# Gathers of the last three layers of a graph network: one wait for a free buffer in place of waits spread over the batch

## The chip, the cores and the metric

The kernel runs on one core of a Trainium2 chip. The metric is device time in microseconds (us). The engines: PE is TensorE (PEld its weight loads), DVE is VectorE, ACT is ScalarE, POOL is GpSimd, SP is SyncE. Engines have queues of their own and are ordered by semaphores alone: `wait_ge(S, n)` holds an engine's queue until semaphore S is at least n, and `then_inc(S, 1)` raises S when the instruction is done. Where this text says that PE *signals*, it means such a raise.

## The reference

Four layers of a graph network over 6250 nodes with 256 features and 106250 edges, sorted by the node that receives. Each layer is x = x + layer(relu(layernorm(x))). Cut to what matters:

```
L0: messages from x[src], edge_attr_4 and an MLP of edge_attr_16; segment_sum; polynomial; batch norm
L1: sums = segment_sum((x @ W_src)[src], dst); mean by degree; batch norm; relu
L2: xp = x @ W;  alpha = leaky_relu(a_src[src] + a_dst[dst] + a_edge);  softmax of alpha over dst
    out = segment_sum(xp[src] * attn, dst); residual; layer norm
L3: the same without a_edge, self loops handled apart
```

What counts here is the step that L1, L2 and L3 share: for each edge a row of a table of nodes is fetched from HBM (the gather), and rows are summed by receiving node.

## The kernel before, in words

Edges are laid out in 880 steps of 128 (`ST`). One indirect DMA on POOL's queue fetches the 128 rows of one step: rows of 256 floats in layer 1 (`k.table`), of 264 floats in layers 2 and 3 (`k.sender_rows`, 8 heads of 32 values and a score). Each layer has 880 such gathers.

**Layer 1, `aggregate` (tag g1).** 110 batches of 8 steps; index, row and one-hot buffers fourfold. PE per batch (`multiply`, L902): transposes edge attributes (`turn`), waits for the one-hot matrices (`sel`) and for all 8 gathers, multiplies one-hot by rows in two halves of four steps (`sums`; L898 and L895). The first half signals `ha`, the second half with the attribute product L887 signals `hb`. DVE (`add`, L975) waits `ha`, adds four steps into `acc`, waits `hb`, adds four. ACT waits `ha` for L923 and `hb` for L929, and makes the one-hot matrices of the batch two further on. PE may not write a half of `psA` again before DVE has added it.

**Layers 2 and 3, `gat` (tags g2, g3).** 55 batches of 16 steps; rows and indices threefold. A body for batch t computes the softmax of t while the sums of batch t-1 are interleaved, a quarter (four steps) at a time. The chain of one body:

- DVE `score` (L2020 to L2024) waits for the 16 gathers of t (`ga`) and for PE's product `sp` (L1874, `spread`, made at the end of the body before). It makes z.
- PE `turn` (L1899) transposes z and signals `zt`; DVE `within` makes running maxima `loc`; PE `edges_of` (L1904, L1905) signals `tb`; ACT and DVE go over the steps (`between`); PE `columns` (L1910) signals `cc`; DVE `differ` makes df; PE `back` (L1926) transposes it and signals `dt`; right after it PE makes `spread` for t+1 and signals `sp`.
- ACT exponentiates (L1994, L1995, after `dt`), DVE weighs the rows (L2088) and goes to `score` of t+1.
- PE's queue in order: sums q0 of t-1, turn, sums q1, edges, sums q2, columns, sums q3, factors, back, spread. So `zt`, `tb`, `cc`, `dt` also say that a quarter of t-1 has been summed. The last reader of the rows of batch t-3 is its sums q3, which `dt` at t-1 covers.

**POOL, layer 1** (`gather`, L861): waits for its indices; before step 0 waits `ha` at t-1, before step 4 `hb` at t-1, that is, until PE has done the first and the second half of batch t-2. **POOL, layers 2 and 3** (`gather`, L1850): before step 0 waits `dt` at t-1; before steps 5, 7 and 9 waits `zt`, `tb`, `cc` at t, which come from body t-1. Each wait is followed by an increment of `go`, for which nobody waits. Buffers that were never used need no wait.

SP's queue loads the indices and, in `gat`, the broadcast rows `bc`, the lines and the heads, each behind its own wait (L1828 to L1844).

Of the kernel before, what the change touches and what calls it, by code (L numbers as in the profile page):

```python
# [93 lines left out]
def triples(eng, times, body):  # L94

    for b in range(3):
        body(b, b, 0)
    with eng.Fori(1, times // 3) as i:
        for b in range(3):
            body(i * 3 + b, b, i)  # L100
    body(times - 1, 0, times // 3)
# [36 lines left out]
def later(i):  # L138

    return not isinstance(i, int) or i > 0  # L140
# [7 lines left out]
def reach(eng, sem, value):  # L148

    if not isinstance(value, int) or value > 0:  # L150
        eng.wait_ge(sem, value)
# [630 lines left out]
def aggregate(nc, k, tag, w_e, att_edge):  # L782
# [8 lines left out]
    with es:  # L791
        S = {n: s[tag + n] for n in names + ["gat0", "gat1", "gat2", "gat3"]}
# [8 lines left out]
        Q = U2 // 2  # L801
# [21 lines left out]
        def eras(eng, body):  # L823

            for t in range(AGE):
                body(t, t, 0, True)
            with eng.Fori(1, (NF - 1) // AGE) as i:
                for c in range(AGE):
                    body(i * AGE + c, c, i, True)
            for t in range((NF - 1) // AGE * AGE, NB2):  # L830
                body(t, t % AGE, t // AGE, t < NF)

        def turns(c, i):

            return i * (AGE // 4) + c // 4

        @block.sync
        def _(sp):
            for o in (0, 1):
                sp.dma_start(we[o * C:(o + 1) * C, :], w_e).then_inc(S["w"], 16)  # L840
            sp.dma_start(av[:, :], att_edge.rearrange("h c -> (h c)").partition_broadcast(P)).then_inc(S["w"], 16)

            def load(t, c, i, left):
                b, n = c % 4, turns(c, i)
                if later(n):
                    sp.wait_ge(r_sem[b], n * per)
                sp.dma_start(idx[b][:, :], k.src_of[:, ds(t * U2, U2)]).then_inc(i_sem[b], 16)
                if left and later(n):
                    sp.wait_ge(S["ha"], t - 3)
                if left and not (isinstance(t, int) and t == NF - 1):  # L850
                    sp.dma_start(f[b][:, :, :], tiles(k.attr[ds(t * (EU * P), EU * P), :])).then_inc(f_sem[b], 16)
                elif left:
                    whole = FT - t * EU
                    sp.dma_start(f[b][:, 0:whole, :], tiles(k.attr[t * EU * P:FT * P, :])).then_inc(f_sem[b], 16)
                    sp.dma_start(f[b][0:LE, whole, :], k.attr[FT * P:E, :]).then_inc(f_sem[b], 16)

            eras(sp, load)

        @block.gpsimd
        def _(g):  # L860
            def gather(t, c, i, left):  # L861
                b, n = c % 4, turns(c, i)
                g.wait_ge(i_sem[b], n * 16 + 16)
                for u in range(U2):
                    if u % Q == 0:
                        if later(n):
                            g.wait_ge(S["hb" if u else "ha"], t - 1)
                        g.sem_inc(S["go"], 1)
                    g.indirect_dma_start(rows[b][:, u, 0:D], None, k.table,  # L869
                                         bass.IndirectOffsetOnAxis(ap=idx[b][:, u:u + 1], axis=0)  # L870
                                         ).then_inc(r_sem[b], 16)

            eras(g, gather)
# [879 lines left out]
def gat(nc, k, tag, edge, own):  # L1753
# [14 lines left out]
    with es:  # L1768
        S = {n: s[tag + n] for n in names + ["ga0", "ga1", "ga2"]}
# [3 lines left out]
        Q = U // 4  # L1773
        HALF = RW // 2

        def sb(name, shape, dt=F32):
            return es.enter_context(nc.sbuf_tensor(tag + name, shape, dt))
# [22 lines left out]
        tb = sb("tb", [1, H, K])  # L1800
# [25 lines left out]
        @block.sync  # L1826
        def _(sp):
            def load(t, b, i):  # L1828
                if later(i):
                    sp.wait_ge(gas[b], i * full)  # L1830
                sp.dma_start(idx[b][:, :], k.src_of[:, ds(t * U, U)]).then_inc(ix[b], 16)
                reach(sp, S["oh"], t)
                sp.dma_start(bc[:, :], k.dst_rows[ds(t * U, U)].rearrange("t e -> (t e)").partition_broadcast(P)
                             ).then_inc(S["bc"], 16)
                if later(i):
                    sp.wait_ge(S["d"], t - 2)
                sp.dma_start(ln[b][:, 0:LU], k.lines[ds(t * U, U), 0:LU].unsqueeze(0).broadcast_to([H, U, LU])
                             ).then_inc(lns[b], 16)
                if edge:
                    sp.dma_start(ae[b][:, :], k.edge_steps[ds(t * U, U), :].rearrange("u (h e) -> h u e", h=H)  # L1840
                                 ).then_inc(aes[b], 16)
                if later(i):
                    sp.wait_ge(S["dt"], t - 2)
                sp.dma_start(hd[b][:, :], k.heads[ds(t, 1), :]).then_inc(hds[b], 16)  # L1844

            triples(sp, NB, load)

        @block.gpsimd
        def _(g):
            def gather(t, b, i):  # L1850
                g.wait_ge(ix[b], i * 16 + 16)
                behind = {0: S["dt"], 5: S["zt"], 7: S["tb"], 9: S["cc"]}
                for u in range(U):
                    if u in behind:
                        reach(g, behind[u], t if u else t - 1)
                        g.sem_inc(S["go"], 1)
                    g.indirect_dma_start(rows[b][:, u, 0:TW], None, k.sender_rows,  # L1857
                                         bass.IndirectOffsetOnAxis(ap=idx[b][:, u:u + 1], axis=0)
                                         ).then_inc(gas[b], 16)

            triples(g, NB, gather)
# [585 lines left out]
```

## Time and profile before

| | us |
|---|---|
| median of 3 runs | 6624.06 (6608.26 to 6634.96) |
| span of the profiled execution | 6720.7 |

The runs' times are taken without the profiler. For the profiled execution the span is the time that is given; it lies 96.6 us (1.5%) above the median.

| engine | busy us | share of the span |
|---|---|---|
| PE | 4346.5 | 65% |
| DVE | 3982.7 | 59% |
| POOL | 3443.0 | 51% |
| PEld | 3322.6 | 49% |
| ACT | 3104.0 | 46% |

How to read the rows below: a row of a timeline is the start in us from the span's start, the duration in us, engine, source line, operation, out<-in, how many instructions it merges, and in brackets how long the engine had been idle before and what ended that. "remote", and the name of a DMA that has nothing to do with the wait, both mean that the wait ended so long after the raising instruction that the profile doesn't connect them. The duration of a POOL row is the time POOL took to hand over the gather, not the transfer.

### The profile page before, as it was taken

The numbers are of one execution on the slowest core, as the hardware profiler recorded it, in microseconds if no ns is written. First come the engines' busy times: TensorE is split into PE (matmuls) and PEld (weight loads), VectorE is DVE, ScalarE is ACT, GpSimd is POOL, SyncE is SP. The second block draws the span as 40 slices with busy tenths as digits, with TensorE's granted clock in tenths as the row PEclk, the third lists the DMA queues.
The fourth block names the chain that finished last, engine by engine and source line by source line (L and its number), as shares of the span: only waits on it lengthen the run. The fifth ranks groups of instructions, "written<-read, shape, count | busy, mean of one in ns | idle before, by whom it ended". The sixth has DMA issues, their size and how long they took to land. (4 is left out here: it accounts for less than half of the span.)

```text
span 6720.7 us, 90392 instructions
## 1 busy us (share of the span) xinstructions
PE 4346.5 (65%) x22227; PEld 3322.6 (49%) x22228; DVE 3982.7 (59%) x8362; ACT 3104.0 (46%) x8998; POOL 3443.0 (51%) x3592
## 2 busy tenths in 40 slices
PE   4799999998666656666555555455565555555556
PEld 3577677776544444444444444444434444444442
DVE  4688778887542222222556566666675666666667
ACT  4688888887253334333343333333333333333332
POOL 2556656664036666666235555555503555555550
PEclk8899999999777777777777777777777777777777
DMA  6333333333034444443233333333303333333332
GB/s 238 85 85 86 87 82 89 88 86 81 29 102 112 112 110 113 112 111 107 81 117 111 107 111 106 108 105 110 103 5 112 105 110 107 105 109 106 105 104 84
DMA packets 677753, 676.59 MB, mean 101 GB/s; under 512 B 457142, under 2 KB 546135, under 8 KB 675851
## 3 DMA queue, kind: packets, MB, share of 16 engines
q0 software_dynamic: 173552, 491.76, 25.8%
q1 hardware_dynamic: 362831, 153.59, 8.9%
q10 hardware_dynamic: 141276, 30.14, 2.2%
q8 instruction: 41, 0.67, 0.0%
q14 instruction: 53, 0.43, 0.0%
HBM read 616.96 MB, written 57.70 MB: 100 GB/s over the span
## 5 line engine op out<-in xcount | busy, mean ns | idle before, releaser
L1857 POOL DMA_INDIRECT g3rows<-sender_rows,g3idx x880 | 841.7, 956 | 849.2 <-issue 270.9
L869 POOL DMA_INDIRECT g1rows<-rows,g1idx x880 | 831.9, 945 | 777.1 <-issue 284.3
L1857 POOL DMA_INDIRECT g2rows<-sender_rows,g2idx x880 | 842.6, 957 | 731.1 <-issue 272.2
L1100 POOL DMA_INDIRECT c0rows<-rows,c0idx x880 | 880.9, 1001 | 583.2 <-issue 463.1
L990 DVE TENSOR_TENSOR acc<-acc,g1psA 128x258 f32 x660 | 279.9, 424 | 953.1 <-remote 729.0
L1129 ACT ACTIVATE c0z<-c0rows,c0sh 128x128 f32<-128x128 f32 x2640 | 793.6, 394 | 0.0
L1891 PE MATMUL g3psA<-g3rows,g3sel 128*128 128x136 f32 x2640 | 502.4, 359 | 428.0 <-ACT g3sel L1968 219.0
L1891 PE MATMUL g2psA<-g2rows,g2sel 128*128 128x132 f32 x2640 | 498.1, 359 | 428.4 <-issue 159.9
L898 PE MATMUL g1psA<-g1rows,g1sel 128*128 128x129 f32 x2640 | 486.8, 353 | 326.6 <-DVE acc L987 196.1
L1891 PEld LDWEIGHTS g3psA<-g3rows,g3sel 128*128 128x128 f32 x2640 | 463.3, 260 | 453.2 <-issue 381.0
L1891 PEld LDWEIGHTS g2psA<-g2rows,g2sel 128*128 128x128 f32 x2640 | 459.9, 264 | 453.1 <-issue 374.3
L898 PEld LDWEIGHTS g1psA<-g1rows,g1sel 128*128 128x128 f32 x2640 | 453.0, 260 | 388.0 <-DVE acc L987 214.1
L1221 PE MATMUL c0psA<-c0prod,c0selk 128*128 128x256 f32 x1760 | 564.3, 403 | 67.9 <-DVE acc L1307 66.4
L1224 PE MATMUL c0psA<-c0prod,c0sel 128*128 128x256 f32 x1760 | 537.6, 388 | 0.2 <-issue 0.2
L1307 DVE TENSOR_TENSOR acc<-acc,c0psA 128x256 f32 x880 | 369.2, 420 | 265.3 <-remote 137.2
L1221 PEld LDWEIGHTS c0psA<-c0prod,c0selk 128*128 128x128 f32 x1760 | 322.8, 195 | 190.4 <-DVE acc L1307 90.9
L2104 DVE TENSOR_TENSOR acc<-acc,g3psA 128x272 f32 x660 | 286.4, 434 | 161.8 <-DMA sender_rows<-p2o 131.6
L2104 DVE TENSOR_TENSOR acc<-acc,g2psA 128x264 f32 x660 | 281.1, 426 | 168.1 <-DMA c0rbf<-rbf_steps 139.6
L1224 PEld LDWEIGHTS c0psA<-c0prod,c0sel 128*128 128x128 f32 x1760 | 343.6, 195 | 50.0 <-issue 0.4
L1117 ACT ACTIVATE c0r<-c0psM 128x512 f32<-128x512 f32 x330 | 187.8, 591 | 233.7 <-remote 181.5
L1138 ACT ACTIVATE c0selk<-c0sel,c0sh 128x128 f32<-128x128 f32 x880 | 280.0, 396 | 0.9
L1963 ACT ACTIVATE g2sel<-iota,dst_in 128x128 f32<-128x128 f32 x880 | 268.6, 387 | 8.3 <-issue 8.1
(439 smaller groups left out, 8668.5 us busy)
## 6 DMA issues: line engine op xcount, KB each, us to landing
g2bc<-dst_rows SPq DMA_DIRECT2D x55, 512.0 KB
g3bc<-dst_rows SPq DMA_DIRECT2D x55, 512.0 KB
g1f<-in_edge_attr SPq DMA_DIRECT2D x103, 256.0 KB
c0rows<-rows,c0idx POOLq DMA_INDIRECT x880
g1rows<-rows,g1idx POOLq DMA_INDIRECT x880
g2rows<-sender_rows,g2idx POOLq DMA_INDIRECT x880
g3rows<-sender_rows,g3idx POOLq DMA_INDIRECT x880
rbf_steps<-prep_extra POOLq DMA_DIRECT2D x7, 1024.0 KB, 8.6
```

Source lines behind the costliest of these rows:

```text
L869: g.indirect_dma_start(rows[b][:, u, 0:D], None, k.table, bass.IndirectOffsetOnAxis(ap=idx[b][:, u:u + 1], axis=0)).then_inc(r_sem[b], 16)
L898: ins = nc.tensor.matmul(to[:, o, n * HALF:(n + 1) * HALF], sel[b][:, u, :], rows[b][:, u, o * HALF:(o + 1) * HALF], start=True, stop=True)
L990: ins = nc.vector.tensor_tensor(to, to, of[:, 0:2, n * HALF:(n + 1) * HALF], ALU.add)
L1100: g.indirect_dma_start(rows[b][:, m, place(n), :], None, k.table, bass.IndirectOffsetOnAxis(ap=idx[b][:, 4 * m + n:4 * m + n + 1], axis=0) ...
L1129: ins = nc.scalar.activation(z[:, m, place(n), 1 + x:5 + x:3, :], row[:, 0:2 + x:1 + x, :], ACT.Copy, scale=sh[b][:, 4 * m + n, 1 + x:2 + x])
L1138: ins = nc.scalar.activation(selk[:, m, n, :], sel[b][:, 4 * m + n, :], ACT.Copy, scale=sh[b][:, 4 * m + n, 0:1])
L1221: nc.tensor.matmul(out, selk[:, m, n, :], prod[:, m, 0, place(n), :, :].rearrange("p k c -> p (k c)"), start=True, stop=False)
L1224: ins = nc.tensor.matmul(out, sel[b][:, 4 * m + n, :], prod[:, m, 1, place(n), :, :].rearrange("p k c -> p (k c)"), start=False, stop=True)
L1307: ins = nc.vector.tensor_tensor(to, to, psA[:, q, u, :], ALU.add)
L1857: g.indirect_dma_start(rows[b][:, u, 0:TW], None, k.sender_rows, bass.IndirectOffsetOnAxis(ap=idx[b][:, u:u + 1], axis=0)).then_inc(gas[b] ...
L1891: ins = nc.tensor.matmul(to[:, o, n * HALF:(n + 1) * HALF], sel[:, u, :], rows[b][:, u, o * HALF:(o + 1) * HALF], start=True, stop=True)
L2104: ins = nc.vector.tensor_tensor(to, to, of[:, 0:2, n * HALF:(n + 1) * HALF], ALU.add)
```

## The change

In layer 1 POOL waits before step 0 alone, for `hb` at t-3: PE is done with batch t-4, which had the same buffer. In layers 2 and 3 POOL waits before step 0 alone, for `dt` at t-1 as before; the waits before steps 5, 7 and 9 go. The increments of `go` that came with the waits go as well.

```diff
@@ aggregate, gather
                 for u in range(U2):
-                    if u % Q == 0:
+                    if u == 0:
                         if later(n):
-                            g.wait_ge(S["hb" if u else "ha"], t - 1)
+                            g.wait_ge(S["hb"], t - 3)
                         g.sem_inc(S["go"], 1)
@@ gat, gather
-                behind = {0: S["dt"], 5: S["zt"], 7: S["tb"], 9: S["cc"]}
+                behind = {0: S["dt"]}
                 for u in range(U):
                     if u in behind:
-                        reach(g, behind[u], t if u else t - 1)
+                        reach(g, behind[u], t - 1)
                         g.sem_inc(S["go"], 1)
```

## Rows read from the trace of the kernel before

**Rows 1.** A group of part 5 of the page: DVE's additions of layer 1

```profile
L990 DVE TENSOR_TENSOR acc<-acc,g1psA 128x258 f32 x660 | 279.9, 424 | 953.1 <-remote 729.0
```

**Rows 2.** Busy time by stage: layers 1, 2, 3; window, its length, engines

```profile
1921.00:3262.00 1341.00, 798.11 (x3704) 588.96 (x3704) 380.37 (x884) 496.34 (x1181) 831.86 (x880) 0.75 0.40 109
3422.00:4902.00 1480.00, 772.77 (x4620) 649.96 (x4620) 927.26 (x1926) 485.28 (x1432) 842.57 (x880) 0.72 0.38 106
5109.00:6592.00 1483.00, 782.31 (x4675) 659.65 (x4675) 943.90 (x1982) 495.65 (x1486) 841.67 (x880) 0.73 0.37 105
```

**Rows 3.** Waits over the span: us in total, times, longest

```profile
DVE g2z L2020 <- remote: 259.4, 47, 14.3
...
PE g1psA L898 <- DMA g1rows<-rows,g1idx: 112.2, 36, 4.2
```

**Rows 4.** Timeline of one batch of layer 2, all engines

```profile
4104.98 0.95 POOL L1857 DMA_INDIRECT g2rows<-sender_rows,g2idx  x1 [0.30 <-issue]
...
4108.34 0.38 DVE L2020 TENSOR_TENSOR g2z<-g2rows,g2psE 128x128 f32<-128x128 f32 x1 [8.10 <-remote]
...
4109.62 0.45 PE L1899 MATMUL g2psT<-ident,g2z 128*128 128x128 f32 x1 [7.48 <-DVE g2z L2024]
...
4110.86 0.94 POOL L1857 DMA_INDIRECT g2rows<-sender_rows,g2idx  x1 [4.93 <-PE g2psT L1899]
...
4113.59 0.35 PE L1905 MATMUL g2psT<-ident,g2loc 128*1 128x128 f32 x1
...
4114.73 1.11 POOL L1857 DMA_INDIRECT g2rows<-sender_rows,g2idx  x1 [1.68 <-PE g2psT L1905]
...
4116.65 0.17 ACT L1988 ACTIVATE g2cin<-g2psT 128x2 f32<-128x2 f32 x1 [0.57 <-PE g2psT L1910]
...
4120.12 0.33 PE L1926 MATMUL g2psT<-ident,g2df 128*128 128x128 f32 x1
...
4120.28 0.68 PE L1874 MATMUL g2psE<-recv,g2oneT 128*128 x16
...
4124.13 0.40 ACT L1994 ACTIVATE g2rows<-g2psT 128x128 f32<-128x128 f32 x1 [7.31 <-DMA c0rbf<-rbf_steps]
...
4126.64 4.47 DVE L2088 TENSOR_TENSOR g2rows<-g2rows,g2psT 128x2048 f32<-128x2048 f32 x2
...
4131.16 0.95 POOL L1857 DMA_INDIRECT g2rows<-sender_rows,g2idx  x1 [0.30 <-issue]
...
4134.90 0.38 DVE L2020 TENSOR_TENSOR g2z<-g2rows,g2psE 128x128 f32<-128x128 f32 x1 [3.78 <-remote]
```

**Rows 5.** Timeline, start of layer 1: 32 gathers with no wait on PE

```profile
1921.11 0.94 POOL L869 DMA_INDIRECT g1rows<-rows,g1idx  x1 [277.75 <-DMA g1idx<-src_of]
...
1937.53 0.60 PE L895 MATMUL g1psA<-g1rows,g1sel 128*128 128x258 f32 x2
...
1938.26 1.34 DVE L990 TENSOR_TENSOR acc<-acc,g1psA 128x258 f32 x3 [8.73 <-remote]
...
1959.85 0.95 POOL L869 DMA_INDIRECT g1rows<-rows,g1idx  x1 [0.30 <-issue]
1966.31 1.34 DVE L990 TENSOR_TENSOR acc<-acc,g1psA 128x258 f32 x3 [26.25 <-remote]
```

**Rows 6.** Timeline amid layer 1: one burst of 12 gathers

```profile
2501.94 0.94 POOL L869 DMA_INDIRECT g1rows<-rows,g1idx  x1 [3.48 <-remote]
...
2506.51 1.03 PE L887 MATMUL g1psS<-g1fT,g1V 128*16 128x512 f32 x2
...
2507.69 0.59 ACT L929 ACTIVATE g1res<-g1psS 16x512 f32<-16x512 f32 x1 [1.13 <-PE g1psS L887]
...
2510.05 0.60 PE L895 MATMUL g1psA<-g1rows,g1sel 128*128 128x258 f32 x2
...
2515.69 0.94 POOL L869 DMA_INDIRECT g1rows<-rows,g1idx  x1 [0.30 <-issue]
...
2519.31 0.60 ACT L923 ACTIVATE g1fT<-g1psF 128x512 f32<-128x512 f32 x1 [11.03 <-remote]
```

## The prediction

> **What bounds the kernel now.** I went from the stage table to the waits and from there to single batches, because no engine is full in the stages that change: layers 1, 2 and 3 take 1341, 1480 and 1483 us, and POOL, which issues the gathers, is busy 832 to 843 us of each, DVE at most 944, PE at most 798 [rows 2]. With its gap of 0.30 us a gather takes POOL 1.25 us (0.95 and 0.30, [rows 4]), so 880 of them fill 1100 us. What holds the stages is a wait, then. In layer 1 DVE stands still 953 us, 729 of them for something the profile cannot name [rows 1]; the score of layer 2 waits 47 times, 259 us in all, for such an unnamed event, while PE waits for gathered rows in layer 1 only 112 us in all [rows 3]. Data isn't short.
>
> The batch of layer 2 shows what is late [rows 4]. PE ends the product `sp` for the next batch at 4120.28 + 0.68 = 4120.96. DVE is done weighing at 4126.64 + 4.47 = 4131.11. Yet the score starts at 4134.90, 13.9 us after PE's end. The other signal of that moment, `dt` (PE's end 4120.45), reaches ACT at 4124.13, 3.7 us late, though ACT had been idle. `zt` (PE's end 4110.07) has POOL going again at 4110.86, and `cc` has ACT going at 4116.65. The difference is what POOL does: at `zt` it stood idle, at `cc` it was 1.9 us into a burst of gathers that began at 4114.73; `dt` and `sp` fall 5.7 and 6.2 us into that burst, and `sp` appears 2.8 us after its last gather has been issued (4131.16 + 0.95 = 4132.11). The batch before gives 2.4 us (4105.93 to 4108.34).
>
> Layer 1 shows the same [rows 6]: a burst of 12 gathers begins at 2501.94. A PE signal at 2507.54 (5.6 us into it) reaches ACT in 0.15 us. The one at 2510.65 (8.7 us into it) reaches ACT at 2519.31, 2.7 us after the end of the last issue (2516.63). So I read: **a signal of PE that comes later than some 5.6 us into an unbroken burst of gathers is held until the burst is over and some 2.4 to 2.8 us more have passed.** What does the holding I can't see.
>
> Is it the wait of POOL on a fresh PE signal that holds it? The start of layer 1 speaks against that [rows 5]: the first 32 gathers wait for no PE signal, they run from 1921.11 to 1960.80, and PE's second half (end 1938.13) is seen by DVE at 1966.31, 28.2 us later. One signal did come through inside that burst: DVE began at 1938.26. The rule has leaks.
>
> **What the change removes.** Three waits and increments per batch of layers 2 and 3 and one in layer 1; POOL has idle time between, so the instructions themselves are worth nothing. What they did was to cut the bursts. In layers 2 and 3 POOL now rests twice around `zt` and `tb`, and the 16 gathers of a period run as 2 and 14. Without them they run as one burst of 16 that starts when `dt` arrives.
>
> *Layers 2 and 3, period after.* Start at the arrival of `dt`, time 0. `sp` comes 0.5 us behind it (4120.96 against 4120.45), POOL's first gather 0.8 us behind it (as 4110.86 behind 4110.07), so `sp` passes. The rows of the next batch were fetched in the burst before. ACT and DVE go on: from ACT's start at 4124.13 to the end of weighing is 7.0 us, so the next score starts at about 7.0 and PE signals `zt` 1.7 us later (4108.34 to 4110.07), at 8.7, which is 7.9 us into the burst: held. The burst lasts 15 x 1.25 + 0.95 = 19.7 us, the holding 2.7 more: `zt` arrives at 0.8 + 19.7 + 2.7 = 23.2. From `zt` to `dt` the trace has 10.4 us (4110.07 to 4120.45), of which PE spends most of the 3.5 up to L1905 on sums that will already have been done during the hold; DVE's addition of a quarter then stands in part of that place. I take 9.5, between 8.6 and 10.4. Period 32.7, from 31.8 to 33.6. The period now is 4134.90 - 4108.34 = 26.6 (stage mean 1480 / 55 = 26.9, first batch included); I count 26.5. That is 6.2 us more in each of 2 x 54 periods, +670 us. At the start of each layer the free burst grows from 21 gathers to 32, 11 x 1.25 = 14 us, +28 for both.
>
> *Layer 1.* A burst of n gathers now costs n x 1.25 plus 2.7 of holding plus 0.7 until POOL starts again (the row 2501.94 came 3.48 after the burst before it): for 12, one and a half batches, 18.4 us, 12.3 a batch; the stage mean is 1341 / 110 = 12.2. After the change a burst is a whole number of batches: 8 gathers give 13.4 a batch, 16 give 11.7, 24 give 11.1. Once a hold ends, PE has one finished batch to report, which frees one buffer, and the next report comes 5 to 9 us later, on either side of the 5.6: bursts of 8 and 16 in turn give (13.4 + 23.4) / 3 = 12.3. I take no change, between -0.5 us a batch (-55) and +1.2 (+130). More depth of prefetch has little to win: at most the 112 us of PE's waits for rows.
>
> *SP's loads* aren't edited, but in layers 2 and 3 the broadcast loads behind `oh` fall into the burst. In layer 1, attribute loads share the DMA engines with the bursts at a mean DMA share of 0.40 [rows 2], with the 2.7 us above. I take nothing, at most 1 us a period (+110), and nothing below zero, since no transfer is made shorter.
>
> Sum: 670 + 28 + 0 + 0, about +700. On the profiled execution 6720.7 becomes about 7420; on the median 6624 becomes **7320 us**.
>
> The Trainium skill, page "TensorE: Matmul & The Clock Gate", section "The cost: per-tile semaphore tail", gives a single increment behind a matmul about 0.06 us. The trace agrees for `zt` and not at all for `sp` with its 13.9 us. By that rule nothing would be held and the sum would be that of the first rival.
>
> **The rivals.**
>
> *Faster, the waits were the brake.* If signals are held because POOL's queue stands at a wait for a newer signal, or if holds fall away for another reason, the period of layers 2 and 3 is the longer of POOL's 16 x 1.25 = 20.0 (20.8 with a restart) and the chain 12.1 (score to `dt`, 4108.34 to 4120.45) + 7.0 = 19.1: 20.8 instead of 26.9, -670 us; layer 1 runs at 10.0 instead of 12.2, -240. Time 5720. For it: each long hold amid the stages ends near a moment at which POOL's queue had such a wait. Against it: the 28.2 us of [rows 5]. It decides from the point where `sp` arrives promptly in a burst of 16. The Trainium skill, page "DMA: Bandwidth & Descriptors", section "Rules for kernel authors", advises issuing a DMA early and waiting for it late; by it this rival is the expected case. The trace has the rows early already.
>
> *Slower, but a signal leaks through.* If `zt`, at 7.9 us into the burst, still passes, `tb` 3.9 us later is held to 23.2, and from `tb` to `dt` remain 6.5 (4113.94 to 4120.45): period 29.7. 2.9 x 108 = +310; 6940. For it: the leak at 1938.26. Against it: the signal at 8.7 us in [rows 6].
>
> *Slower still.* Bursts of 8 alone in layer 1 (+130), 33.6 in layers 2 and 3 (+100), loads that stretch the burst: 7500 to 7650.
>
> *It does nothing.* Index loads or SP's queue could pace the gathers as the waits did. Indices wait for the gathers of the same buffer alone, loaded long before: 6624.
>
> **How the numbers follow.** Forecast (31.8 to 33.6 a period, 7170 to 7500): 0.66. Leak (6900 to 7170): 0.11. Still slower, above 7500: 0.06. Nothing: 0.04. Faster: 0.13. The range reaches from the leak's 6940, with 20 for layer 1, to 7500: 0.77 plus the edge of the still slower one. The measurement of this kernel can tell about 0.5% from no change: faster 0.13, same 0.04, slower 0.83.
>
> **What the profile after would show.** In layers 2 and 3: POOL rows in runs of 16 with one idle stretch of about 12 us each, ended by L1926; PE L1899 done some 8.7 us after `dt`, and DVE L2033 starting about 14 us after that; `score` no longer waiting for an unnamed event; stages of 1800 to 1850 us. In layer 1 bursts of 8 and 16 and a stage within 1285 to 1470. I'm wrong if L2033 follows L1899 promptly (then the rival at 5720 or the leak), if POOL's runs are shorter than 16, or if layer 1 moves by more than its bounds.

## The result

The changed kernel takes 7297.9 us (median of 4 runs, 7291.9 to 7312.0) against 6620.8 (4 runs, 6608.3 to 6635.0) of the kernel before: ratio **1.1024**, 95% interval 1.1008 to 1.1041, 677 us slower. The forecast was 7320, in a range from 6920 to 7500, with 0.83 on slower. The profiled execution of the changed kernel spans 7297.2 us, 576.5 more than that of before. The difference to the 677 is mostly layer 0, whose code is the same in both: its gathers ran for 1406 us here and for 1461 in the profiled execution of before. A further part lies in layers 2 and 3: a batch takes 26.4 us in that execution of before, and 26.1 in e_g1only below, where these layers are the same.

Busy time by stage after, for layers 1, 2 and 3, to be laid beside [rows 2] (window, its length, PE, PEld, DVE, ACT and POOL with their instructions, granted clock, DMA share, GB/s):

```profile
1866.00:3185.00 1319.00, 743.22 (x3704) 539.80 (x3704) 381.30 (x885) 497.81 (x1183) 831.58 (x880) 0.76 0.41 111
3343.00:5154.00 1811.00, 847.59 (x4620) 719.05 (x4620) 926.53 (x1927) 483.85 (x1433) 844.26 (x880) 0.67 0.31 87
5355.00:7168.00 1813.00, 876.73 (x4675) 741.60 (x4675) 941.95 (x1982) 494.14 (x1486) 842.95 (x880) 0.67 0.31 86
```

Layer 1 lost 22 us, layers 2 and 3 gained 331 and 330. POOL and DVE have the same work as before within 1%; the stages are longer by waiting. PE is busy 75 and 94 us longer for the same number of instructions, at a granted clock of 0.67 in place of 0.72 and 0.73: what became slower also made PE slower. The waits say who stands still (us in total, times, longest):

```profile
ACT g2tf L1975 <- remote: 910.4, 54, 43.8
ACT g3tf L1975 <- remote: 887.3, 54, 45.3
DVE acc L990 <- remote: 707.4, 94, 25.7
DVE g2ob L2057 <- ACT g2tb L1976: 568.8, 53, 13.2
...
POOL g2rows L1857 <- PE g2psT L1926: 420.8, 34, 12.8
```

The `score` of layer 2, which stood in [rows 3] with 259 us behind an unnamed event, is gone from the list. In its place ACT waits once a batch, 54 times, for PE's transposes of the ends (L1905, the signal `tb`), and DVE waits for ACT behind it. POOL stands 12 to 13 us a batch for `dt` (L1926). `acc` L990 is layer 1, as in [rows 1].

One batch of layer 2, all engines (start and length in us, engine, line; in brackets the idle time before and what ended it), to be laid beside [rows 4]:

```profile
4103.70 0.33 PE L1926 MATMUL g2psT<-ident,g2df 128*128 128x128 f32 x1
4104.83 0.94 POOL L1857 DMA_INDIRECT g2rows<-sender_rows,g2idx  x1 [12.29 <-PE g2psT L1926]
...
4110.97 0.38 DVE L2020 TENSOR_TENSOR g2z<-g2rows,g2psE 128x128 f32<-128x128 f32 x1
...
4112.67 0.42 PE L1899 MATMUL g2psT<-ident,g2z 128*128 128x128 f32 x1
...
4114.80 0.35 DVE L2033 SCALAR_TENSOR_TENSOR g2zz<-g2psT,mask,g2ae 128x128 f32<-128x128 f32 x1 [2.06 <-remote]
...
4116.56 0.27 PE L1905 MATMUL g2psT<-ident,g2loc 128*1 128x128 f32 x1
...
4118.16 1.62 PE L1891 MATMUL g2psA<-g2rows,g2sel 128*128 128x132 f32 x12 [1.33 <-issue]
...
4123.87 0.95 POOL L1857 DMA_INDIRECT g2rows<-sender_rows,g2idx  x1 [0.30 <-issue]
...
4128.02 0.27 ACT L1975 ACTIVATE g2tf<-g2psT 1x128 f32<-1x128 f32 x1 [16.34 <-remote]
...
4130.06 1.01 PE L1910 MATMUL g2psT<-ones,g2inc 1*128 1x1 f32 x4 [9.84 <-ACT g2inc L1981]
4131.63 3.01 PE L1891 MATMUL g2psA<-g2rows,g2sel 128*128 128x132 f32 x12 [0.56 <-DVE acc L2101]
...
4136.40 0.47 PE L1926 MATMUL g2psT<-ident,g2df 128*128 128x128 f32 x1
```

Read it by the two signals. `zt` (L1899) is done at 4113.09, 8.3 us into POOL's burst, and DVE has it at 4114.80, 1.7 late. `tb` (L1905) is done at 4116.83. POOL's last issue ends at 4124.82; ACT starts at 4128.02, 11.2 us after PE was done and 3.2 after the burst. From `dt` (end 4104.03) to the next `dt` (4136.87) are 32.8 us. Over the whole of layers 2 and 3 a batch takes 32.4 us on average, against 26.4 before. POOL's issues in layer 2 come in 45 runs of 16 and 8 of 15 with a single one ahead, after a first run of 32. (Here and below a gap under 1 us doesn't end a run, or burst.) PE isn't standing while `tb` is on its way: at 4118.16 it starts twelve more sums. The profile models the ends of matmuls, so it can't tell a signal that was sent late from one that travelled long; "held" in this text means only that it arrived late.

### The profile page after: what moved, and what is told of

Same layout as the page of the kernel before. It is cut to its first block and busy times, and to the rows that moved or that the text cites. A ratio compares the mean times of both kernels' runs of the same rounds, so it can differ in the third digit from the quotient of the medians.

```text
span 7297.2 us, 89918 instructions
## 1 busy us (share of the span) xinstructions
PE 4441.1 (61%) x22227; PEld 3404.0 (47%) x22228; DVE 3976.5 (54%) x8362; ACT 3096.0 (42%) x8998; POOL 3465.9 (47%) x3592
## 2 busy tenths in 40 slices
DMA packets 677752, 676.58 MB, mean 93 GB/s; under 512 B 457142, under 2 KB 546135, under 8 KB 675851
## 5 line engine op out<-in xcount | busy, mean ns | idle before, releaser
L1100 POOL DMA_INDIRECT c0rows<-rows,c0idx x880 | 900.2, 1023 | 510.0 <-issue 465.7
L990 DVE TENSOR_TENSOR acc<-acc,g1psA 128x258 f32 x660 | 279.7, 424 | 930.1 <-remote 707.4
L1891 PE MATMUL g3psA<-g3rows,g3sel 128*128 128x136 f32 x2640 | 555.0, 385 | 355.3 <-ACT g3sel L1968 187.1
L1891 PE MATMUL g2psA<-g2rows,g2sel 128*128 128x132 f32 x2640 | 541.4, 380 | 349.1 <-ACT g2sel L1968 194.9
L1891 PEld LDWEIGHTS g3psA<-g3rows,g3sel 128*128 128x128 f32 x2640 | 507.6, 282 | 394.4 <-issue 326.9
L1891 PEld LDWEIGHTS g2psA<-g2rows,g2sel 128*128 128x128 f32 x2640 | 496.9, 283 | 386.2 <-issue 321.6
L898 PE MATMUL g1psA<-g1rows,g1sel 128*128 128x129 f32 x2640 | 440.2, 329 | 218.4 <-DVE acc L987 161.6
L898 PEld LDWEIGHTS g1psA<-g1rows,g1sel 128*128 128x128 f32 x2640 | 409.4, 239 | 275.5 <-DVE acc L987 194.0
L1975 ACT ACTIVATE g2tf<-g2psT 1x128 f32<-1x128 f32 x55 | 14.6, 266 | 913.9 <-remote 910.4
L1975 ACT ACTIVATE g3tf<-g3psT 1x128 f32<-1x128 f32 x55 | 14.6, 266 | 890.8 <-remote 887.3
L1910 PE MATMUL g2psT<-ones,g2inc 1*128 1x1 f32 x220 | 55.1, 350 | 522.5 <-ACT g2inc L1981 517.8
```

Source lines behind the costliest of these rows:

```text
L898: ins = nc.tensor.matmul(to[:, o, n * HALF:(n + 1) * HALF], sel[b][:, u, :], rows[b][:, u, o * HALF:(o + 1) * HALF], start=True, stop=True)
L990: ins = nc.vector.tensor_tensor(to, to, of[:, 0:2, n * HALF:(n + 1) * HALF], ALU.add)
L1100: g.indirect_dma_start(rows[b][:, m, place(n), :], None, k.table, bass.IndirectOffsetOnAxis(ap=idx[b][:, 4 * m + n:4 * m + n + 1], axis=0) ...
L1891: ins = nc.tensor.matmul(to[:, o, n * HALF:(n + 1) * HALF], sel[:, u, :], rows[b][:, u, o * HALF:(o + 1) * HALF], start=True, stop=True)
L1910: ins = nc.tensor.matmul(psT[0:HU, brought][:, a:a + 1], inc[0:1, a, :], k.ones[0:1, 0:1], start=True, stop=True)
```

## The experiments

What had to be told apart: which of the two edits costs, whether it is POOL's bursts that hold TensorE's signals, what in a burst does so, and what ends a hold. Times of one row of the table were taken on one chip beside the kernel before, whose own time differed by 1.4% between the groups of rows, so a time is compared with the one in its own row. The middle column is the mean batch of layers 2 and 3, from the trace.

```
kernel                                   us (median)  us a batch   before   ratio (95% interval)
after                                    7297.9       32.4, 32.4   6620.8   1.102 (1.101 to 1.104)
e_g1only     layer 1's edit alone        6621.6       26.1, 26.1   6627.4   0.999 (0.998 to 1.001)
e_gatonly    layers 2 and 3 alone        7314.1       32.5, 32.6   6627.4   1.105 (1.102 to 1.107)
e_nonpe      waits on DVE, ACT instead   6736.4       27.2, 27.1   6627.4   1.017 (1.015 to 1.019)
e_spearly    spread moved forward        6722.2       26.8, 27.1   6627.4   1.016 (1.013 to 1.018)
e_pooldirect plain DMAs on POOL          5796.4       18.4, 18.7   6625.1   one run
e_sphw       plain DMAs on SP            5777.3       18.4, 18.7   6625.1   one run
e_half       8 gathers in place of 16    6107.3       21.1, 21.7   6625.1   one run
e_two8       one wait, zt at 8           7234.4       31.9, 31.2   6625.1   1.092 (1.090 to 1.094)
e_land8      own rows at 8               6856.5       27.8, 28.0   6714.2   1.023 (1.020 to 1.026)
e_land08     own rows at 8 and at end    6580.8       25.4, 25.2   6714.2   0.980 (0.978 to 0.982)
e_fours      waits at 4, 8, 12           6639.3       25.7, 26.3   6714.2   0.989 (0.987 to 0.990)
e_land7b     own rows but the last one   6816.6       27.8, 27.4   6710.4   1.015 (1.012 to 1.017)
```

**Which edit.** Each hunk of the change alone, on the kernel before.

> The kernel before with layer 1's part of the change alone. If a burst of n gathers costs n x 1.25 + 3.4 us and layer 1 goes over to bursts of 8 and 16, its stage stays within 1285 to 1360 us and the time within 20 us of before minus 20: 6600. If the change's loss sat partly in layer 1, the time would lie over 6700.

> The kernel before with the part of the change in layers 2 and 3 alone. If all of the loss is the longer burst there: 7300 to 7320, 32.5 us a batch instead of 26.5. If half of it came from layer 1: near 6950.

Both came out as expected, the first with 1.6 us over the 6620 that I had given it. Layer 1's edit changes nothing that the runs can tell, though its bursts did change, from 68 of 12 to 24 of 8 and 35 of 16: gathers of the layer ran for 1307 us against 1319 in e_gatonly, where that layer is as before. All of the loss is in layers 2 and 3.

**Is it that POOL waits for TensorE?** The kernel before, with its three inner waits moved to signals of DVE and ACT.

```
-                behind = {0: S["dt"], 5: S["zt"], 7: S["tb"], 9: S["cc"]}
+                behind = {0: S["dt"], 5: S["loc"], 7: S["tr"], 9: S["cs"]}
```

> The kernel before, but in layers 2 and 3 POOL's waits before steps 5, 7 and 9 are for DVE's and ACT's signals of about the same moments (loc, tr, cs) instead of PE's zt, tb, cc; bursts are cut as before, and POOL waits for no fresh signal of PE but dt. If the length of a burst is what holds PE's signals: as before, 6580 to 6660. If POOL's wait for a fresh PE signal held them, sp arrives at once and the period falls from 26.5 towards 20.8: near 6000.

The waits were no brake by being waits on TensorE: had they been, this kernel would run near 6000. It is 1.7% slower than before instead, also outside the 6580 to 6660 that I expected. Its bursts are 4 and 12, and in 22 batches of layer 3 again 16, because a wait cuts only where its signal comes late. The signals of PE are late in it too:

```profile
4116.17 0.45 PE L1899 MATMUL g2psT<-ident,g2z 128*128 128x128 f32 x1 [0.93 <-issue]
...
4118.27 0.94 POOL L1857 DMA_INDIRECT g2rows<-sender_rows,g2idx  x1 [0.30 <-issue]
...
4121.87 0.35 DVE L2033 SCALAR_TENSOR_TENSOR g2zz<-g2psT,mask,g2ae 128x128 f32<-128x128 f32 x1 [5.28 <-remote]
```

`zt`, done at 4116.62, is seen at 4121.87: again between 2 and 3 us behind the last issue (end 4119.21).

It is PE's signals alone that are late. In the three layers of the changed kernel, 145 waits were ended by a signal that DVE or ACT had raised for another engine more than 5.6 us into a burst, none of them more than 0.02 us late. Of the 444 ended by such a signal of PE, 386 came over 1 us late.

**Can `sp` be taken out of the hold?** The kernel before, with `spread(t + 1)` moved from the end of the batch to right behind `edges_of(t)`.

```
                 edges_of(t)
+                if not last_one:
+                    spread(t + 1, at)
...
                 back(t)
-                if not last_one:
-                    spread(t + 1, at)
```

> The kernel before, but PE makes the product sp for the next batch right behind edges_of, some 4 us after zt, instead of behind back. Theory (any PE signal late in a burst is held to its end): sp then passes early, the score starts 7.0 us after dt, and now zt, 8.7 us after dt, is held to the burst's end at about dt + 14.4; the period falls by the 1.8 us between score and zt: 24.8, -190 us, 6430. If only sp or its instruction were subject to holding: period 19 to 20.8, 5900 to 6050. If sp wasn't what the score waited for: 6620.

This missed, by 4.5% on the side of slower. `sp` was held only some 2.4 us, as meant, and yet nothing was won. The trace shows what took its place:

```profile
4102.47 1.01 POOL L1857 DMA_INDIRECT g2rows<-sender_rows,g2idx  x1 [3.57 <-PE g2psT L1910]
...
4110.03 0.95 POOL L1857 DMA_INDIRECT g2rows<-sender_rows,g2idx  x1 [0.30 <-issue]
...
4112.97 0.38 DVE L2020 TENSOR_TENSOR g2z<-g2rows,g2psE 128x128 f32<-128x128 f32 x1 [1.37 <-DMA g2rows<-sender_rows,g2idx]
...
4114.25 0.30 PE L1899 MATMUL g2psT<-ident,g2z 128*128 128x128 f32 x1 [0.82 <-issue]
...
4116.34 0.95 POOL L1857 DMA_INDIRECT g2rows<-sender_rows,g2idx  x1 [0.30 <-issue]
...
4120.06 0.35 DVE L2033 SCALAR_TENSOR_TENSOR g2zz<-g2psT,mask,g2ae 128x128 f32<-128x128 f32 x1 [5.40 <-remote]
```

The burst of 12 begins with gather 9, which waits for `cc`. The score needs the seventh of the twelve, landed 2.0 us after its issue (4110.98 to 4112.97), and `zt` then falls 12.1 us into the burst and is held for its end: 4114.55 to 4120.06. I had left out that the rows now come last, and that a signal taken out of a hold puts the next one into it.

**What in a burst holds?** Three kernels, all made from the changed one. The first:

```
-                    g.indirect_dma_start(rows[b][:, u, 0:TW], None, k.sender_rows, ...).then_inc(gas[b], 16)
+                    g.dma_start(rows[b][:, u, 0:TW], k.sender_rows[u * P:(u + 1) * P, :]).then_inc(gas[b], 16)
```

> The changed kernel with one edit: in layers 2 and 3 the 16 gathers of a batch are plain DMAs of 16 x 128 consecutive rows, issued by POOL in the same places, so the lookup by index is left out (the rows fetched are the wrong ones, as many and as large as before). It tells whether it is the indexed form that holds PE's signals. My theory (POOL's issuing of an unbroken burst of about 20 us holds them, whatever the form): if a plain issue takes POOL about as long as the 1.25 us of a gather, tb is held 10 to 14 us as in the changed kernel, a batch takes 31 to 33 us, the stages 1750 to 1850 us, the whole 7250 to 7350. Rival, only the indexed form holds: L1905 reaches ACT within 1 us, and a batch takes the longer of POOL's 20 us and the chain of about 19: 20 to 21.5 us, the whole 5900 to 6100. If a plain issue is much shorter than 1 us, the burst ends before zt is due and both give about 20 us a batch; the time of one issue then says so.

The second has the same DMAs on SP's queue, and POOL's loop of gathers is gone:

```
                 sp.dma_start(hd[b][:, :], k.heads[ds(t, 1), :]).then_inc(hds[b], 16)
+                reach(sp, S["dt"], t - 1)
+                sp.wait_ge(ix[b], i * 16 + 16)
+                for u in range(U):
+                    sp.dma_start(rows[b][:, u, 0:TW], k.sender_rows[u * P:(u + 1) * P, :]).then_inc(gas[b], 16)
```

> As the one before, but the 16 plain DMAs of a batch stand in SP's queue, behind the same wait for dt, and POOL issues nothing in layers 2 and 3. The bytes moved are the same. My theory (it is POOL's issuing that holds the signals, not the bytes on their way): no signal of PE in these layers is more than 1 us late, L1905 is followed by ACT L1975 at once, a batch takes the 19 to 21 us of the chain, the whole 5850 to 6100. Rival, the traffic of a batch's rows holds them, whoever issues it: zt or tb late by 5 us or more, a batch 28 to 33 us, the whole 6900 to 7350.

The third issues every other gather, and counts on its semaphore accordingly:

```
-                for u in range(U):
+                for u in range(0, U, 2 if later(i) else 1):
```

> The changed kernel, but from batch 3 on of layers 2 and 3 only the even eight of a batch's 16 gathers are issued (the other rows keep what the buffer held). POOL's burst is half as long, 8 x 1.25 = 10 us from dt + 0.8 to dt + 10.8. My theory (a hold lasts until the burst is over and 2.4 to 2.8 us more): zt at dt + 8.7 comes no later than dt + 13.5, everything behind it is prompt, a batch takes 19 us if zt leaks through to 24 us if it is held to the end, the stages 1050 to 1300 us, the whole 5800 to 6350. Rival, the signals are late for a reason that has nothing to do with the burst's length (the first of a kind after dt, TensorE's own queue, the clock): tb stays 10 us or more late, and a batch takes 30 us or more, the whole 7000 to 7300.

My theory that POOL's issuing holds the signals "whatever the form" falls with the first of them, and the rival named there holds: **it is the indexed DMAs**. The times lie below what that rival gave (5900 to 6100, 20 to 21.5 us a batch), and e_sphw below its 5850, since a plain issue is short: POOL needs 8.8 us for sixteen, and the chain alone, 18.4 us, sets the pace. With plain DMAs on POOL:

```profile
3906.44 8.79 POOL L1857 DMA_DIRECT2D g2rows<-sender_rows  x16 [9.73 <-PE g2psT L1924]
...
3914.50 0.42 PE L1897 MATMUL g2psT<-ident,g2z 128*128 128x128 f32 x1
...
3915.07 0.35 DVE L2031 SCALAR_TENSOR_TENSOR g2zz<-g2psT,mask,g2ae 128x128 f32<-128x128 f32 x1 [0.49 <-PE g2psT L1897]
```

and with eight gathers:

```profile
3905.25 0.95 POOL L1857 DMA_INDIRECT g2rows<-sender_rows,g2idx  x1 [10.26 <-PE g2psT L1926]
...
3913.03 0.42 PE L1899 MATMUL g2psT<-ident,g2z 128*128 128x128 f32 x1
3914.14 0.95 POOL L1857 DMA_INDIRECT g2rows<-sender_rows,g2idx  x1 [0.30 <-issue]
3915.22 0.35 DVE L2033 SCALAR_TENSOR_TENSOR g2zz<-g2psT,mask,g2ae 128x128 f32<-128x128 f32 x1 [2.21 <-remote]
```

In both, `zt` is done 8.5 and 8.2 us into a burst of 8.8 and 9.8 us. Behind the plain DMAs DVE starts 0.15 us later, behind the gathers 1.77 us later. Bursts of 8.8 us are short, but layer 2 opens with a longer one, 32 issues without a wait, in both forms. In the changed kernel (40.0 us, from 3343.50):

```profile
3356.82 2.14 PE L1874 MATMUL g2psE<-recv,g2oneT 128*128 x15
3370.42 0.38 DVE L2020 TENSOR_TENSOR g2z<-g2rows,g2psE 128x128 f32<-128x128 f32 x1 [14.20 <-remote]
```

and with plain DMAs on POOL:

```profile
3362.40 17.57 POOL L1857 DMA_DIRECT2D g2rows<-sender_rows  x32 [127.36 <-DMA g2idx<-src_of]
3378.17 0.38 DVE L2018 TENSOR_TENSOR g2z<-g2rows,g2psE 128x128 f32<-128x128 f32 x1 [3.06 <-PE g2psE L1872]
```

`sp` is done 15.5 us into the first and reaches DVE 11.5 us later, amid the burst; it is done 15.7 us into the second (3378.06) and is there 0.1 us later. Of PE's signals in layer 2, 272 with plain DMAs on POOL and 277 with them on SP, none is more than 0.02 us late. The traffic is the same: 677753 packets and 676.58 MB with plain DMAs on POOL, 677752 and 676.58 MB in the changed kernel. So neither the bytes nor the number of packets hold the signals. What isn't told apart is how: the plain DMAs leave out the lookup, but they also fetch consecutive rows in place of scattered ones, and an issue takes POOL 0.56 us in place of 0.96. No kernel here looks up consecutive rows by index. And I can't see what POOL does in either.

With eight gathers a batch takes 21.1 and 21.7 us, inside the 19 to 24 expected, and `tb`, 11.2 us late at the median of layer 2 in the changed kernel, is prompt (0.01). So the length of the burst sets the hold, not the place behind `dt`.

**How much cutting is needed?** The kernel before with a single inner wait.

```
-                behind = {0: S["dt"], 5: S["zt"], 7: S["tb"], 9: S["cc"]}
+                behind = {0: S["dt"], 8: S["zt"]}
```

> The kernel before with one edit in layers 2 and 3: POOL's waits inside a batch, at gathers 5, 7 and 9, become a single one, for zt at gather 8. So a dose between the bursts of 2 and 14 of before and the 16 of the changed kernel. My theory: the first eight run from dt + 0.8 to dt + 10.8; zt, ready at dt + 8.7, is 7.9 us in and either leaks through in some 2 us or is held to dt + 13.4; the second eight start there and last to dt + 21 to 23.5; tb is 2 us into them and passes, cc at their 6th us is at the edge, dt is ready within them and held to their end + 2.6: a batch 25 to 27.5 us, the whole 6450 to 6750, near the kernel before and far from the changed one. Rival, the loss of the changed kernel comes from dropping each of the three waits (two of the three dropped, so about two thirds of the loss): 7050 to 7100.

Both expectations missed; it costs nearly as much as dropping all three. Layer 2 has 38 bursts of 16 and 15 of 8. The row of gather 8 says why:

```profile
4109.60 0.94 POOL L1857 DMA_INDIRECT g2rows<-sender_rows,g2idx  x1 [0.62 <-issue]
...
4118.34 0.94 POOL L1857 DMA_INDIRECT g2rows<-sender_rows,g2idx  x1 [0.30 <-issue]
...
4122.15 0.27 ACT L1975 ACTIVATE g2tf<-g2psT 1x128 f32<-1x128 f32 x1 [16.30 <-remote]
```

`zt` had just leaked through when POOL came to wait for it, so the gap is 0.62 us where 0.30 is the usual one, and `tb` behind it is held to 2.9 us after the sixteenth issue (4119.28). So a wait seems to be worth only the gap that it makes. That can be tried without any wait on TensorE: POOL waits for the rows of its own gathers, in e_land8 with the first three added lines of this diff, in e_land08 with all five.

```
                     if u in behind:
                         reach(g, behind[u], t - 1)
                         g.sem_inc(S["go"], 1)
+                    if u == 8:
+                        g.wait_ge(gas[b], i * full + full // 2)
+                        g.sem_inc(S["go"], 1)
...
+                g.wait_ge(gas[b], i * full + full)
+                g.sem_inc(S["go"], 1)
```

> The changed kernel with one wait added in layers 2 and 3: ahead of a batch's gather 8, POOL waits until the rows of its own gathers 0 to 7 have landed. No engine's signal is waited for, TensorE's least of all; all the wait does is to make a gap of about 2 us in the burst of 16 (a row lands some 2 us after the end of its issue), where the single wait for zt at gather 8 made one of 0.62 us only, because zt had just leaked through, and lost 9.2%. My theory (what ends a hold is a real gap on POOL, whatever makes it): bursts of 8; zt comes at dt + 8.7 to 13.4, tb soon after, cc 4 us into the second burst, dt either passes or is held to its end + 2.6 (dt + 25.4); a batch takes 24 to 27 us, the whole 6350 to 6680. Rival A, what the waits of the kernel before did was to hold POOL back until TensorE had reported, and a gap at another place is worth nothing: 31 to 34 us, the whole 7150 to 7350 or, with 2 us a batch added to it, 7500. Rival B, a gap of 2 us is too short to release anything: the same 7300 to 7500.

> As the one before, and POOL also waits for the rows of gathers 8 to 15 before it goes on to the next batch, so that no burst can be longer than 8, also where dt comes early. POOL alone then needs 16 x 1.25 + 2 x 2 = 24 us a batch. My theory: if dt passes inside the second burst of the kernel before this one, the bursts there merge into longer ones and this kernel is the faster, 24 to 26 us a batch, 6350 to 6570; if dt is held there anyway, both take the same time within 0.5%. Rival: a gap has nothing to do with it, 7150 to 7500.

> The kernel before with its three inner waits at gathers 4, 8 and 12 (for zt, tb and cc as before) and not at 5, 7 and 9, in layers 2 and 3. My theory: the first four run from dt + 0.8 to dt + 5.8, zt at dt + 8.7 is prompt; four run from there to 14.5, tb at 11.4 is prompt and so its wait makes no gap; cc at 15.5, 6 us in, is at the edge of being held. If it passes, 12 gathers run in one piece from 9.5 to 24.5 and dt is held to 27; if it is held to 22, the last four end at 27.3 and dt passes at 25.5. A batch takes 25.5 to 27.5 us, the whole 6510 to 6740. Rival, that it is each wait's own hold-up of POOL that costs, so that waits later in the batch cost less: 23 to 25 us, 6200 to 6450.

The wait for own rows at gather 8 wins back most of the loss (1.102 to 1.023), though it stays above the range that I gave it. Both waits together **beat both kernels**: 0.980 of the kernel before. No signal of TensorE is waited for but `dt`, so it is the gap that counts. The second wait is worth about 4% (0.980 against 1.023), by the first of the two branches that I had named: 25.4 and 25.2 us a batch where 24 to 26 was said, though the whole, 6580.8, lies 11 us over its range. Without it, `dt` passes inside the second burst in some batches, the next batch's gathers join on, and one such stretch costs about 15 us (9 bursts of 16 in each layer, and 2.4 to 2.8 us more a batch over 54 batches; the `score` at 3611.31 came 34.8 us after the one before it, at 3576.47):

```profile
3588.49 0.76 PE L1877 MATMUL g2psE<-recv,g2oneT 128*128 x16
...
3606.48 0.94 POOL L1860 DMA_INDIRECT g2rows<-sender_rows,g2idx  x1 [2.62 <-DMA g2rows<-sender_rows,g2idx]
...
3611.31 0.38 DVE L2023 TENSOR_TENSOR g2z<-g2rows,g2psE 128x128 f32<-128x128 f32 x1 [13.00 <-remote]
```

`sp`, done at 3589.25, reached DVE 22.0 us later, across a gap of 2.62. With both waits no burst is longer than 8, and a batch looks like this:

```profile
4119.72 1.09 POOL L1860 DMA_INDIRECT g2rows<-sender_rows,g2idx  x1 [2.74 <-DMA g2rows<-sender_rows,g2idx]
...
4128.08 0.70 PE L1915 MATMUL g2psT<-ones,g2inc 1*128 1x1 f32 x4
4128.65 0.95 POOL L1860 DMA_INDIRECT g2rows<-sender_rows,g2idx  x1 [0.30 <-issue]
...
4131.37 0.17 ACT L1993 ACTIVATE g2cin<-g2psT 128x2 f32<-128x2 f32 x1 [5.65 <-remote]
4132.21 0.94 POOL L1860 DMA_INDIRECT g2rows<-sender_rows,g2idx  x1 [2.62 <-DMA g2rows<-sender_rows,g2idx]
...
4143.93 0.38 DVE L2025 TENSOR_TENSOR g2z<-g2rows,g2psE 128x128 f32<-128x128 f32 x1 [2.73 <-DMA g2rows<-sender_rows,g2idx]
4144.69 1.04 POOL L1860 DMA_INDIRECT g2rows<-sender_rows,g2idx  x1 [2.79 <-DMA g2rows<-sender_rows,g2idx]
```

POOL now sets the pace: from 4119.72 to 4144.69 are 25.0 us, 16 issues and two gaps. One signal a batch, `cc` (L1915), is held, here 2.6 us (4128.78 to 4131.37) and 4.2 at the median of layer 2, and the score waits for its rows. e_fours came out within its range, at 0.989: waits on the old signals at better places gain about half as much.

**Can the gaps be shorter?** Each of the two waits leaves out the gather issued last.

```
-                                         ).then_inc(gas[b], 16)
+                                         ).then_inc((gbs if u % 8 == 7 else gas)[b], 16)
+                    if u == 8:
+                        g.wait_ge(gas[b], i * 224 + 112)
...
+                g.wait_ge(gas[b], i * 224 + 224)
-                    sp.wait_ge(gas[b], i * full)
+                    sp.wait_ge(S["z"], t - 2)
```

> The kernel with the two waits for POOL's own rows (ahead of gather 8 and at a batch's end), which took 24.9 us a batch and 0.980 of the time before, with gaps of 2.6 to 2.8 us on POOL. Here each of the two waits leaves out the last gather issued and asks only for the seven ahead of it (gathers 7 and 15 count on a semaphore of their own; SP's reload of the index buffer waits for z of three batches before, in place of the rows themselves). The gap should shrink by one issue, 2.65 - 1.25 = 1.4 us, and at no moment amid a layer has every issued gather landed. My theory (a gap in POOL's issuing ends a hold, and a new hold starts 5.6 us into the next burst): 16 x 1.25 + 2 x 1.4 = 22.8 us a batch for POOL, about 22.2 for the chain as it stood in that kernel, so 22.8 to 24, the whole 0.947 to 0.968 of the kernel before. Rival A (a hold ends only when every issued gather has landed, and the 2.4 to 2.8 us after the last issue are just that landing): the holds run on through the gap, bursts act as one of 16 or longer, a batch takes 28 to 34 us, 1.03 to 1.12. Rival B (the hold ends a fixed 2.4 to 2.8 us after the last issue of a burst, gap or not, so a burst of 8 with this gap holds 1.2 us longer into the next): one held signal a burst, each some 1.2 us later: 24.5 to 26 us, 0.975 to 1.00.

It is slower, 1.015, between the two rivals, and the run tells less than I had hoped, since the gaps came out uneven: about 56 between 1.2 and 1.6 us, 22 up to 2.4, and more above. At some, the awaited rows landed late, with SP's loads landing in the same stretch:

```profile
4137.76 0.95 POOL L1860 DMA_INDIRECT g2rows<-sender_rows,g2idx  x1 [0.30 <-issue]
4142.50 0.95 POOL L1860 DMA_INDIRECT g2rows<-sender_rows,g2idx  x1 [3.79 <-DMA g2rows<-sender_rows,g2idx]
```

(SP's reload was moved with it, so what made them late stays open.) What the gaps do can be counted all the same, over both layers. Of the signals held when a gap between 1.2 and 2.4 us began, 28 came through near it and 28 stayed held beyond it. At gaps of 2.4 to 2.8, 100 came through and none stayed. So it looks as if a gap must outlast something that takes about 2 us. More than half of the batches take 22 to 26 us from `score` to `score`, others up to 34.6, and the mean is 27.8 and 27.4.

**What a hold ends with.** The same count over five kernels gives the time from the end of a burst's last issue to the arrival of a signal held until then, with the landing of the last gather's rows for comparison (medians; here a gap of 0.5 us ends a burst):

```
issues in the burst        4            8            12       14      16
signals counted            85, 99       104, 111     61       16      89
arrival, us after the end  1.2, 1.0     1.8, 1.7     2.4      2.7     2.95
rows landed, us after      1.8, 1.8     1.8, 1.8     1.7      1.7     1.6
(kernel)                   fours,       fours,       before   before  after
                           spearly      land08
```

The rows land 1.6 to 1.8 us after the last issue whatever the burst; the signals come about 0.15 us later for each issue of the burst more, roughly 0.6 + 0.15 x n. The 32 gathers of [rows 5] fit: the last issue ended at 1960.80, the signal came at 1966.31, 5.5 us later, and 0.6 + 0.15 x 32 is 5.4. Layer 1 gives the same with rows of 256 floats: 1.75 us behind 8 issues (21 holds) and 3.0 behind 16 (38) in the changed kernel, 2.7 behind 12 (68) in the one before, 5.4 behind the first 32 in both. So it isn't the landing that frees them. It looks like a backlog that each gather adds to; that is argued from the fit, nothing shows the backlog itself.

## Why the prediction was right, and where it wasn't

*The bound.* Right. A wait sets the stages, and the change moved the wait, not the work.

*Start and period.* The first burst grew to 32 as said. `sp` comes promptly. The score starts 6.9 us after `dt` (4104.03 to 4110.97; 7.0 was said), `zt` is done 9.1 after it (8.7). The period is 32.4 on average (32.7, from 31.8 to 33.6, was said), and the two stages grew by 661 us (698 were said).

*The step that failed* is "`zt` ... is held". `zt`, 8.3 us into the burst, leaked through 1.7 us late, by 1.6 at the median of the layer, and the one held was `tb`. DVE's L2033 followed PE's L1899 by 1.7 us where about 14 was said, and the prediction itself had named a prompt L2033 as a sign of being wrong. That was the mechanism of the rival "a signal leaks through", which gave 29.7 us a batch and 6940. (From its own 26.5 us that is 3.2 us a batch and not 2.9, and with the 28 us of the longer first bursts about 7000.) So the forecast's time was right by way of a wrong signal, and that is luck: holding the wrong one adds 3.0 us to a batch (32.7 against 29.7), and two terms of the rival's sum, which the forecast shares in part, were too small by 3.2 together. The rival's mechanism was right with a wrong price.

The rows already spoke for the leak. In [rows 4] `dt`, 5.7 us into the burst, reached ACT at 4124.13, 8 us before the burst's last issue ended, so it wasn't held to the end, and `sp` behind it was. [rows 5] and [rows 6] have the same order: of the signals due more than some 5 us into the burst, the first passes and the next is held. I had counted one leak, and gave this rival 0.11.

Those two terms are these. The release came 24.0 us after `dt` (4128.02), not 23.2: one issue took 1.23 us, and from the last issue to ACT's start were 3.2 us and not 2.7 (2.95 at the median of the table above, for bursts of 16). And from `tb` to `dt` there were 8.9 us (4128.02 to 4136.87), not 6.5; at the medians of layer 2, 8.6 after the change and 6.5 before it. That is PE's clock. PE had stood idle 9.84 us during the hold, since `columns` waited for ACT and the fourth quarter of the sums stands behind `columns` in PE's queue. The stretches of this batch, from `dt` on, show the clock:

```profile
4104.00:4118.00 14.00, 7.08 (x48) 5.96 (x44) 11.15 (x19) 7.55 (x20) 10.12 (x11) 0.76 0.46 131
4118.00:4130.00 12.00, 2.06 (x14) 1.65 (x14) 1.44 (x7) 0.93 (x5) 5.29 (x6) 0.75 0.32 85
4130.00:4137.00 7.00, 6.38 (x34) 5.54 (x35) 4.00 (x11) 0.37 (x4) 0.00 (x0) 0.50 0.00 0
```

and the kernel before, in the batch of [rows 4], the row of the fourth quarter's twelve sums and the stretch that has them:

```profile
4117.59 1.62 PE L1891 MATMUL g2psA<-g2rows,g2sel 128*128 128x132 f32 x12 [0.98 <-DVE acc L2101]
...
4117.00:4121.00 4.00, 3.38 (x35) 2.88 (x35) 3.03 (x9) 0.00 (x0) 2.93 (x4) 1.00 0.41 110
```

After the idle stretch the granted clock is 0.50, the lower level of 1.2 GHz; in the kernel before it is 1.00, and the twelve sums take 1.62 us in place of 3.01. From the first of these sums to the end of `dt` the changed kernel takes 5.2 us (4131.63 to 4136.87), and the kernel before 2.9 (4117.59 to 4120.45), which is nearly the whole difference. The way from `tb` to these sums is the same in both, 3.6 us. I had noted that a hold lets PE finish its sums. It finished only those ahead of `columns`, and I left out that it then goes on at half the clock.

*Layer 1.* Right: 0 was said, and the profiled stage is 22 us shorter, in bounds of -55 and +130. Bursts of 8 and 16 in turn, as said.

*SP's loads.* Taken at nothing. Nothing in the runs contradicts it, and nothing measured it.

*From the profile to the median.* The sum of +700 was set against the profiled 6720.7; the medians differ by 677. The profiled spans differ by 576.5, for the reason given with the result.

*The rival "faster, the waits were the brake".* It named 20.8 us a batch once nothing is held. The plain DMAs show that chain free of holds: 18.4 and 18.7 us a batch, and 5796 us in all, near its 5720, though with layer 1 unchanged, for which it had counted 240 us less. But its mechanism is refuted by e_nonpe and e_land08: waits don't hold, the gaps that they make free. The Trainium skill, page "DMA: Bandwidth & Descriptors", section "Rules for kernel authors", advises issuing early and waiting late. The plain DMAs of e_pooldirect, issued in one piece, hold no signal; no run issues them later for comparison. For indexed ones on this kernel the runs speak against it: issuing them earlier, in one piece, costs 10%, and two added waits gain 2%. The page "TensorE: Matmul & The Clock Gate" of the Trainium skill, section "The cost: per-tile semaphore tail", has a formula that gives, as an estimate for one matmul and one increment, 0.06 us. The traces agree where no indexed burst runs (0.02 us at most in e_pooldirect), and not within one (up to 22 us in e_land8, 28.2 in [rows 5]).

## What to carry to other kernels

A wait in POOL's queue that looks superfluous may be what breaks a long run of indexed DMAs, and TensorE's signals come late in such a run. Before removing one, look in the timeline at how long POOL's unbroken runs become, and at which consumer of a PE signal starts 1 to 3 us after their last issue with an unnamed releaser. If runs must be cut, a wait of POOL on its own landed rows does it at a place that one chooses: here at every eighth gather, where a gap of 2.6 us stands against the 1.8 us after which held signals arrive. And count what an idle PE loses in clock behind the hold: here 2.1 to 2.4 us a batch.

## What was not expected of the hardware

- PE's signals, and not DVE's or ACT's, are late in runs of indexed DMAs. Plain DMAs with as many packets from the same queue hold none (272 signals, 0.02 us at most), and the batch falls from 32.4 to 18.4 us.
- The first signal due some 8 us into a run often passes with a delay of 1.6 us (the median of `zt` in the changed kernel, in e_half and in e_two8), the next is held to its end. `dt` in [rows 4] passed 3.7 us late in the same way, and `sp` in the opening burst of layer 2 after 11.5 us, 13 us before that burst's end. What decides which passes isn't known.
- The arrival after the run's end grows with its length, from 1.0 or 1.2 us for 4 issues to 2.95 for 16 and 5.5 for 32, while the rows land after 1.6 to 1.8.
- A gap of 2.4 us or more let every signal through in the last kernel; gaps of 1.2 to 2.4 only half of them. In e_land8, where bursts of 16 remain, 14 of 124 signals stayed held across gaps of 2.4 to 2.8, as `sp` above. So the length of a gap isn't all that counts.
